# First layer of a four-layer image mixer: more 3x3 taps on TensorE in 64x64 blocks, two GpSimd chains, and reordered work for softmax and displacement weights

## The reference, cut to what matters

```python
z    = groupnorm(x)
x1   = gelu(layernorm(depthwise_conv3x3(z) + dw_b))      # per pixel over 256 channels
off  = x1 @ off_w + off_b       # per pixel: 16 groups x 9 points x (x, y)
mask = softmax(x1 @ mask_w + mask_b)   # over the 9 points of a group
xp   = z @ in_w + in_b
# out[pixel, group, c] = sum over 9 points of mask * bilinear(xp, point + off)
x    = x + out @ out_w + out_b
```

## Time and profile before

| | before |
|---|---|
| median of 3 runs | 810.39 us (804.23 to 815.72) |
| the profiled execution | 810.63 us |
| its span | 808.9 us |
| busy PE / DVE / ACT / POOL | 682.7 / 547.3 / 324.1 / 348.8 us |
| chain that ended last | PE 51%, DVE 30%, POOL 8%, ACT 4% |
| mean granted TensorE clock | 0.945 |

### The profile page before, as it was taken

One profiled execution on the slowest core, in us unless ns is written; L12 is line 12 of the kernel. 1 busy time (PEld: TensorE's weight loads), 2 busy tenths in 40 slices (PEclk: granted clock), 3 DMA queues, 4 the chain that ended last, 5 costly groups with the idle time before them and its releaser, 6 DMA issues.

```text
span 808.9 us, 8778 instructions
## 1 busy us (share of the span) xinstructions
PE 682.7 (84%) x3418; PEld 368.2 (46%) x3418; DVE 547.3 (68%) x627; ACT 324.1 (40%) x475; POOL 348.8 (43%) x196
## 2 busy tenths in 40 slices
PE   1968677887987799999879899499789989989796
PEld 0665356776983365444211456244352324325232
DVE  5897989994637234500145424469999999995598
ACT  2704820002010434000336211259897968763163
POOL 5630019998950533000000000235999888960060
PEclk9998879998998799999979999899899999999989
DMA  5039400374001913930203700200000000000002
GB/s 185 0 64 140 59 0 1 50 117 83 1 2 52 285 65 130 350 132 0 105 26 133 245 13 0 83 0 1 0 1 1 2 2 1 1 1 1 13 1 104
DMA packets 37766, 49.51 MB, mean 61 GB/s; under 512 B 2644, under 2 KB 26004, under 8 KB 36396
## 3 DMA queue, kind: packets, MB, share of 16 engines
q1 hardware_dynamic: 37724, 48.94, 22.5%
HBM read 28.19 MB, written 10.49 MB: 48 GB/s over the span
## 4 chain that ended last, share of the span: by engine, by line
PE 51%; DVE 30%; POOL 8%; ACT 4%; issue 3%; DMA 3%; SPq 0%; DVEq 0%; POOLq 0%; ACTq 0%
DVE psum L413 12%; PE psum L873 8%; PE psum L811 6%; PE psum L1110 4%; PE psum L983 4%; PE psum L844 3%; PE psum L1082 3%; POOL arena L2053 3%; PE psum L771 3%; POOL arena L2056 3%; PE psum L969 2%; PE psum L891 2%; PE psum L730 2%; PE psum L947 2%; PE psum L853 1%
## 5 line engine op out<-in xcount | busy, mean ns | idle before, releaser
L413 DVE SCALAR_TENSOR_TENSOR psum<-arena,psum 128x1024 f32<-128x1024 f32 x123 | 158.5, 1289 | 3.9
L2129 POOL TENSOR_TENSOR arena<-arena 128x1024 f32<-128x1024 f32 x76 | 151.4, 2023 | 11.0 <-ACT arena L1887 10.4
L811 PE MATMUL psum<-arena 128*128 128x128 f32 x800 | 96.7, 282 | 12.6 <-DVE arena L491 11.0
L811 PEld LDWEIGHTS psum<-arena 128*128 128x128 f32 x800 | 91.5, 145 | 17.9 <-DVE arena L491 13.2
L491 DVE TENSOR_TENSOR arena<-arena,psum 128x2048 f32<-128x2048 f32 x37 | 82.3, 2282 | 19.3 <-PE psum L811 12.0
L1887 ACT ACTIVATE arena<-arena 128x1024 f32<-128x1024 f32 x80 | 91.7, 1179 | 4.5 <-POOL arena L2129 4.4
L2088 POOL MEMSET arena<- 128x864 f32 x1 | 0.8, 836 | 194.8 <-DVE arena L1497 194.8
L1082 PE MATMUL psum<-arena 64*64 64x512 f32 x648 | 81.6, 617 | 2.2 <-ACT arena L1929 1.8
L873 PE MATMUL psum<-arena 128*128 128x512 f32 x144 | 63.8, 602 | 0.0
L491 POOL TENSOR_TENSOR arena<-arena 128x2048 f32<-128x2048 f32 x13 | 47.0, 3645 | 4.6 <-PE psum L811 4.5
L998 PE MATMUL psum<-arena 128*128 128x512 f32 x96 | 43.0, 611 | 4.3 <-ACT arena L1675 4.3
(11 more groups left out here) (238 smaller groups left out, 1213.5 us busy)
## 6 DMA issues: line engine op xcount, KB each, us to landing
arena<-fc_w_dram SPq DMA_DIRECT2D x10, 1024.0 KB, 12.1
bounce<-arena SPq DMA_DIRECT2D x32, 256.0 KB, 2.1
arena<-bounce SPq DMA_DIRECT2D x32, 256.0 KB, 5.6
arena<-arena SPq DMA_DIRECT2D x16, 480.0 KB
arena<-x_dram SPq DMA_DIRECT2D x4, 512.0 KB, 5.1
out_dram<-arena SPq DMA_DIRECT2D x3, 512.0 KB, 2.6
arena<-sp_w_dram SPq DMA_DIRECT2D x1, 1152.0 KB
arena<-arena SPq DMA_DIRECT2D x8, 140.0 KB
```

What stands on the lines that cost most here:

```text
L413: return eng.scalar_tensor_tensor(dst, tap_view(t, a, b), wt, filter_acc, ALU.mult, ALU.add)
L811: m = pe.matmul(psum[:, 4 * hf + xx // 4, xx % 4 * P:(xx % 4 + 1) * P], prods[n % NB][:, xx * P:(xx + 1) * P], ident, start=(first and xx ...
L2129: g.tensor_tensor(dst, dst, tap_tmp(n), ALU.add).then_inc(s_ta, 1)
```

## The change

What it does, in order of the program:

- Taps: TensorE does all nine taps of plane (1, 0) and the first two of plane (1, 1), in four 64x64 blocks per tap (44 matmuls). ACT moves both sums out with their bias (`evacuate_sums`, eight instructions of 64x512). DVE does nine taps of (0, 0) and seven of (1, 1). ACT writes one plane of `Z` itself and makes nine tap matrices. The banks of `xp` are now 2, 3, 6, 7, and the turning of the planes runs in the order of the banks 4, 5, 0, 1, 2, 3, 6, 7, waiting for each evacuation by itself.
- Plane (0, 1): ACT writes the first two products straight into two sums, POOL adds the others to them in turn and adds the two at the end (eight additions). POOL also writes planes 1 and 3 of `Zc`, which ACT did.
- The nine batch-norm operations stand behind the layer-norm writes.
- Softmax: TensorE sums the nine exponentials with the identity (L797 of the changed kernel, three sums of nine matmuls, 96, 32 and 128 columns); DVE inverts out of PSUM and normalises the mask of half 0 in two pieces. ACT takes one exponential between two hat operations.
- Terms of half 0: three buffers `wk` in place of two, and the last two products stand ahead of the normalised mask of half 1.
- Weights of half 1: the four corner terms first, each writing what no earlier term has written straight into `Wd1`; the clearing goes.
- Products: POOL has 24, 25, 26, 29, 31, ... 45, 49, thirteen as before.

The diff, cut to its core:

```diff
-PE_TAPS = {(1, 0): 3, (1, 1): 4}
+PE_TAPS = {(1, 1): 2, (1, 0): 9}
+PE_SUMS = {(1, 1): 2, (1, 0): 6}
-XPROJ_BANKS = [6, 7, 4, 5]
+XPROJ_BANKS = [2, 3, 6, 7]
+TURN_ORDER = [4, 5, 0, 1, 2, 3, 6, 7]
+TERM_ORDER = [(ky, kx) for ky in (0, 2, 1) for kx in (0, 2, 1)]
+NEW_AND_OLD = {(0, 0): [((0, 3), (0, 3))],
+               (0, 2): [((1, 3), (0, 3)), ((0, 1), (0, 3))],
+               (2, 0): [((0, 3), (1, 3)), ((0, 3), (0, 1))],
+               (2, 2): [((1, 3), (1, 3)), ((0, 1), (0, 3)), ((1, 3), (0, 1))]}
-POOL_PRODUCTS = (24, 26, 28, 30, 32, 34, 36, 38, 40, 42, 44, 46, 49)
+POOL_PRODUCTS = (24, 25, 26, 29, 31, 33, 35, 37, 39, 41, 43, 45, 49)
...
             for (k, b), taps in PE_TAPS.items():
-                for yh in range(2):
-                    for tap in range(taps):
-                        m = pe.matmul(psum[:, DW_ACC[k, b] + yh, :], tap0[:, tap, :], tap_image(k, b, tap)[:, 16 * yh:16 * yh + 16, :],
-                                      start=(tap == 0), stop=(tap == taps - 1))
+                if b == 0:
+                    pe.wait_ge(s_z, 3)
+                for tap in range(taps):
+                    for c, half, bank, to in QUARTERS3:
+                        rows = slice(64 * half, 64 * half + 64)
+                        m = pe.matmul(psum[64 * to:64 * to + 64, PE_SUMS[k, b] + bank, :], tap0[rows, tap, rows],
+                                      tap_image(k, b, tap)[rows, 16 * c:16 * c + 16, :], start=(tap == 0), stop=(tap == taps - 1))
                 m.then_inc(s_dwt, 1)
...
-                if n == 2:
-                    pe.wait_ge(s_x1, 1)
-                if n >= 4:
+                if n < 4:
+                    pe.wait_ge(s_act0, 2 if n < 2 else 3)
+                else:
                     pe.wait_ge(s_xpe, n - 3)
...
+            def sum_over_taps(hf, lo, hi, bank):
+
+                for k in range(K2):
+                    m = pe.matmul(psum[:, bank, 0:hi - lo], ident, mask[:, hf, k, lo:hi], start=(k == 0), stop=(k == K2 - 1))
+                m.then_inc(s_om, 1)
...
+            for tap in range(PE_TAPS[1, 1], 9):
+                if tap > PE_TAPS[1, 1]:
+                    me.upto(tap_n)
+                ins = depthwise_tap(1, 1, tap)
+                if tap < 8:
+                    tap_n = me.add(ins)
+                    if tap > PE_TAPS[1, 1]:
+                        evacuate_xproj(evacuated)
+                        evacuated += 1
+            ins.then_inc(s_x1, 1)
+            for n in range(evacuated, 8):
+                evacuate_xproj(n)
...
-            me.link(v.tensor_reduce(sm_r[:, 0], mask[:, 0].rearrange("p k g -> p g k"), AX.X, ALU.add))
-            me.link(v.reciprocal(sm_t[:, 0], sm_r[:, 0]))
...
+            pool.wait_ge(s_z, 3)
+            for i in (1, 3):
+                g.tensor_scalar(Zc[:, i], X.rearrange("p h b q -> p (h b) q")[:, i], grs[:, i:i + 1], gnb[:, i:i + 1],
+                                ALU.mult, ALU.add).then_inc(s_zc, 1)
+            for tap in range(2, 9):
                 pool.wait_ge(s_dwp, tap + 1)
...
+                dst = x1_chains[tap % 2]
+                g.tensor_tensor(dst, dst, dw_tmp[tap % 3], ALU.add).then_inc(s_dwa, 1)
+            pool.wait_ge(s_dwa, 7)
+            g.tensor_tensor(x1_chains[0], x1_chains[0], x1_chains[1], ALU.add).then_inc(s_dwa, 1)
...
-            me.add(g.memset(Wd1, 0.0))
             pool.wait_ge(s_mask, 2)
...
+            for ky, kx in TERM_ORDER:
+                window = Wd1[:, kx:kx + 3, ky:ky + 3, :]
+                fresh, *covered = NEW_AND_OLD.get((ky, kx), [None, ((0, 3), (0, 3))])
+                if fresh:
+                    i, j = fresh
+                    me.add(term_product(window[:, i[0]:i[1], j[0]:j[1], :], ky, kx, i, j))
+                for i, j in covered:
+                    me.add(term_product(part(wk1, i, j), ky, kx, i, j))
```

More of the change, by code:

```diff
@@ L746, in _ @@
                 m.then_inc(s_xp, 1)
[L748 to L752 removed]
+            pe.wait_ge(s_x1, 2)
+            pe.wait_ge(s_dwa, L0_ADDS)
+            for t in TURN_ORDER:
+                if t in XPROJ_BANKS:
+                    pe.wait_ge(s_xpe, 5 + XPROJ_BANKS.index(t))
                 for u in range(2):
@@ L1238, in group_norm @@
                 v.tensor_copy(gq[:, 0, :], mv[:, :, 0]).then_inc(s_gn_stats, 1)
+                if layer == 0:
+                    dve.wait_ge(s_const, 80)
+                    v.tensor_scalar(bnv, col("bn_v", 0, 6), GN_EPS, None, ALU.add).then_inc(s_bnv, 1)
                 dve.wait_ge(s_gn_means, layer + 1)
@@ L1258, in group_norm @@
                     return
-                for i in range(4):
+                for i in range(3 if layer == 0 else 4):
                     v.tensor_scalar(z_inner(i), Xi[:, i], grs[:, i:i + 1], gnb[:, i:i + 1], ALU.mult, ALU.add).then_inc(s_z, 1)
@@ L1322, in _ @@
+            ins.then_inc(s_x1, 1)
+            for n in range(evacuated, 8):
+                evacuate_xproj(n)
             tiles = psum[:].rearrange("p t (u c) -> p (t u) c", c=C)
-            for t in range(XX):
-                dve.wait_ge(s_x1t, t // 2 + 1)
-                n = me.add(v.bn_stats(ln_st[:, t, :], tiles[:, t, :]))
+            for turned_n, bank in enumerate(TURN_ORDER):
+                dve.wait_ge(s_x1t, turned_n + 1)
+                for t in (2 * bank, 2 * bank + 1):
+                    n = me.add(v.bn_stats(ln_st[:, t, :], tiles[:, t, :]))
@@ L1666, in group_norm @@
                     a.activation(bnsd, bnv, ACT.Sqrt).then_inc(s_bnsd, 1)
+                    for tap in range(4, 9):
+                        ins = tap_matrix0(tap)
+                    ins.then_inc(s_taps, 1)
                 act.wait_ge(s_gn_coef, layer + 1)
```

196 lines of the change are left out of this document (99 added, 97 removed).

## The result

| | before | after |
|---|---|---|
| median (lowest to highest of 4 runs each, one chip; a fifth run of after took 782.59) | 813.06 us (804.23 to 816.89) | 785.61 us (784.53 to 790.58) |
| ratio, 95% interval | | 0.970 (0.961 to 0.979) |
| the profiled execution, its span | 810.63, 808.9 us | 790.58, 788.8 us |
| busy PE / DVE / ACT / POOL | 682.7 / 547.3 / 324.1 / 348.8 us | 684.1 / 533.2 / 327.8 / 339.2 us |
| chain that ended last | PE 51%, DVE 30%, POOL 8% | PE 54%, DVE 26%, POOL 8% |

The change is faster by 3.0%. The time lies 4.4 us under the predicted 790.0.

A forecast was written before the change was run, and what follows sets the result against it. The first layer's chain of waits was taken as the bound (PE and DVE alternating, then POOL's weights and PE's products), later layers only shifting: 810.6 - 6.1 - 6.9 - 7.5 = 790 us, 8-in-10 range 783 to 800.

The forecast's parts named there:

- Front: First layer up to the layer-norm statistics: they start at 46.9 in place of 53.01, -6.1 us (bounds -3 and -7.5).
- Eleven taps are then 11.3 + 3.0 = 14.3 us: done at 31.8: TensorE's taps in the first layer's front: 11.3 us warm plus 3.0 for starting out of idleness, done at 31 to 33.
- Softmax and terms: First layer, softmax sums through terms of half 0: end at 122.6 in place of 129.5, -6.9 us (bounds -2 and -8).
- T: End of the softmax terms in the first layer, predicted at 122.6 in place of 129.5; the sampling is counted from it.
- PE is cold in the softmax: Rival, softmax: half-clock sums take 5.4 us each, terms end 5.3 us later, total 795 us; chance 18%.
- Sampling: First layer, after the terms: ends 101.9 us behind their end in place of 109.4, -7.5 us (bounds -4 and -8).
- small pieces bring nothing: Rival, POOL's weights of half 1: extra instructions eat the saved additions, product 26 comes 6 us later, 796 us; chance 14%.
- held by something else: Rival, second half of the sampling: not PE's restart holds it, 3 to 4 us of 7.5 are missing, 794 us; chance 12%.
- Slower (3%): Rival, front: 64x64 blocks don't overlap, 3.4 us per tap, PE's taps end 25 us later, 815 us; chance 3%.
- the sign for being right was under 1: Sign for being right, sampling: PE's pause between the halves is under 1 us.
- near 47: Sign for being right, front: the layer-norm statistics start near 47 us.
- about 14: Sign for being right, front: PE's tap blocks take about 14 us.

The follow-up runs named there:

- two-buffer: Changed kernel with two buffers for the softmax terms instead of three: 788.72 us in a single run.
- the mask experiment: Changed kernel with the last two term products put back behind the normalised mask of half 1: 788.01 us, ratio 0.971 to the kernel before.
- old weight chain: Changed kernel with POOL's weights of half 1 made as before (cleared first, nine full products, nine full additions): 792.90 us, ratio 0.977 to the kernel before.
- the kernel before kept busy: Kernel before the change plus 16 unread matmuls in TensorE's pause ahead of half 1: 808.82 us, ratio 0.994 to the kernel before.
- the full-array taps: Changed kernel with TensorE's eleven taps as full-array matmuls instead of 64x64 blocks: 795.11 us, ratio 0.978 to the kernel before.
- the repetition: The changed kernel, unedited, measured and profiled a second time: 787.13 us, ratio 0.973 to the kernel before.

## Why the prediction was right, and where it was off

**Front, -6.1 against -9.0: one term mis-sized.** The failing step is "Eleven taps are then 11.3 + 3.0 = 14.3 us: done at 31.8". The 11.3 for blocks at full clock is right; the 3.0 for a restart of TensorE was read from one execution of before and taken as fixed. The blocks took 11.62, and over all eleven profiles of kernels that have them 11.34 to 12.78: 0.0 to 1.5 over 11.3. The 28 passes of before, 15.20 in the earlier trace rows, took 14.11 in the next profile. All that follows the taps was right: 15.1 us predicted from there to the statistics, 15.1 measured, and after the last evacuation nothing is late. POOL's two planes took 2.4 us, not 3.2, and its chain ended at 42.75, just under the 43 to 44 predicted. The two chains of additions and the place of the nine batch-norm operations were not undone by themselves, so what they are worth is not shown.

**Softmax and terms, -6.9 against -7.3: the size right, two of its reasons not.** The first mask came 1.9 earlier, not 1.4, because the sums of 96 and 32 columns take 2.14 and 2.32 us, 0.12 to 0.13 us a pass, and not the 3.2 that I scaled from two single passes. Three buffers and the moved products I booked for the terms; the two-buffer and the mask experiment show that T hardly depends on them, since TensorE paces the terms, and that the buffer pays behind T. The rival "PE is cold in the softmax" (18%, 5.3 us) came true as a fact and not in its price. Its own working doesn't close either: three sums of 5.4 us from 92.7 end at 108.9, not at 107.4. The windows of after:

```profile
88.00:90.00 2.00, 1.53 (x13) 1.40 (x12) 1.93 (x4) 2.00 (x4) 0.00 (x0) 0.79 0.01 4
90.00:94.00 4.00, 3.94 (x18) 3.95 (x19) 3.87 (x4) 3.63 (x6) 0.10 (x1) 0.50 0.02 6
94.00:96.00 2.00, 2.00 (x8) 1.52 (x7) 2.00 (x3) 2.00 (x3) 0.00 (x0) 0.51 0.00 0
```

The first two sums were at full clock, and only the third and two microseconds of terms were not: 1.3 us, of which I had booked 0.8.

**Sampling, -7.5 against -7.6: right but for the place of one pause.** Second mask at T - 3.1 (T - 3.5 predicted), hats 8.07 (8.1), their products and additions 43.2 from 117.9 to 161.1 (43.1), product 24 done at T + 51.9 (51.35, and 51.7 with its signal), pauses of 1.23 us in all (0.6 and 0.6), 24 products in 42.14, 1.76 each (1.75). The place of the pause was not right: it was predicted ahead of products 27 and 28, for DVE, and stands ahead of 26, for POOL. Products 25 and 26 were done 0.5 and 0.6 us later than predicted, and by the prediction's own numbers 26 was ready at T + 59.0 where TensorE wanted it at 58.7, a wait that it didn't count. That the sum of the pauses came out is luck. The rival "small pieces bring nothing" is refuted by the old weight chain (+6.3), the rival "held by something else" by the kernel before kept busy, whose 43.89 us are the 46.75 without the restart. Nine profiles of kernels that keep the change's weights of half 1, places and three buffers end the sampling at T + 101.7 to T + 102.0.

The page TensorE: Matmul & The Clock Gate of the Trainium skill (Part 4) says that transposes don't count as busy for the clock in the same way. Here TensorE did nothing but transposing matmuls from 172.4 to 214.5, with the granted clock at 1.00 in every window of this stretch, and in the kernel before it rose at about 198 in the midst of them: for these transposes the measurement decides against the page.

**Slower (3%)**: the blocks do overlap, 88 passes in 11.6 us, 1.06 per tap; the full-array taps took 1.93.

**The later layers** shift only in the repetition, as predicted. In the profiled execution they take 574.3 us and not 570.0, and its 790.6 us fit the predicted 790 by two errors that cancel, which is luck: 3.9 us more gained in the first layer, and 4.3 us lost behind it, with the long half clock of the second layer. The median of 785.6 is what the first layer alone says: 810.6 - 24.4 = 786.2.

**The signs.** Two of the signs that the prediction named for being wrong were seen, and both were small: a clock of 0.50 during the third sum (1.3 us), and TensorE idle ahead of product 26 (1.23 us, where the sign for being right was under 1). The statistics at 44.0 and blocks of 11.6 us missed "near 47" and "about 14" on the good side. Product 24 was waiting when TensorE came to it, and 25 products at the pace of the second half are 43.9 us (44 predicted).

## What to carry to other kernels

When work moves onto an engine that stands ahead of the next stage, its own duration there is what counts, not the load taken from the other engine: the front came 8 to 9 us sooner with eleven taps in blocks and nothing sooner with them on the full array. A buffer, a moved instruction or a product on another engine pays where something waits behind it, which may be far from where it was put: ask who starts when it is done. Count the restart of TensorE as a range, not as the number of one profile. Where a pause can't be removed and a long stretch of TensorE follows, it is worth trying to fill it with matmuls nobody reads: this took 2.9 us out of the kernel before, likely some 4 out of the second layer, and nothing that the whole time shows out of the softmax. A stretch whose length changes by 10 us between profiles must be looked at in more than one of them.

## What was unexpected

- TensorE's half clock behind one and the same pause of 3.1 us in the second layer lasted from 384 to 403 in one profile of the changed kernel and to 395 in another; with some 3 us more of it between 424 and 440 in the first, the stretch between the marks differs by 6.2 us. What decides it is open.
- The eighteen passes of 32 columns took no less (2.32, 2.19 us) than those of 96 (2.14 us): from 32 to 96 columns a pass costs 0.12 us whatever its width, here with a weight load each. The page TensorEngine Tiling (Array Packing) of the Trainium skill (Instruction Overhead) gives about 60 cycles as the floor; at 2.4 GHz that would be an estimate of 0.025 us, and the passes here take nearly five times as long.
- An instruction of nine elements per partition on DVE took 2.58 us in place of 0.23 while POOL was at a masked hat. It started at 111.80 and ended at 114.38, and POOL's second hat ended at 114.35.
